# A causal attention stage with routing: from half items of eight heads to one whole item a step

## The reference

```
x = x + self_attention(norm(x))                     # stage 1, causal, 16 heads of 16
x = x + cross_attention(context, norm(x))           # stage 2
x = x + _L0_ffn_ref(norm(x), ...)                   # stage 3: the one that is changed
x = x + rotation_attention(norm(x)); x = x + wide_cross(norm(x)); x = x + moe(norm(x))   # stages 4 to 6

def _L0_ffn_ref(x, ...):
    q_in = k_in = rope(x)                           # r1 = x1*cos - x2*sin, r2 = x1*sin + x2*cos, on neighbours
    q, k, v = q_in @ Wq.T + bq, k_in @ Wk.T + bk, x @ Wv.T + bv
    attn = softmax(causal(q k^T / 4))               # 16 heads of 16, 100 x 100 for each of 32 items
    x1 = layer_norm(x + (attn v) @ out_proj.T + b, ln1_w, ln1_b)
    gates = softmax(x1 @ gate_w.T + gate_b); top_idx = top 2 of 8
    moe_out = sum over the two of gate * (x1 @ expert_w.T + expert_b)
    return layer_norm(x1 + moe_out, ln2_w, ln2_b)
```

## Time and profile before

| what | us |
|---|---|
| median of three runs | 3509.99 |
| lowest and highest | 3508.03, 3511.72 |
| profiled execution, own time | 3483.03 |
| profiled execution, span | 3481.2 |
| PE busy | 3282.1 (94%) |
| DVE busy | 1841.8 (53%) |
| ACT busy | 1636.2 (47%) |
| POOL busy | 1556.1 (45%) |

### The profile page before, as it was taken

One profiled execution on the slowest core, in us unless ns is written; L12 is line 12 of the kernel. 1 busy time (PEld: TensorE's weight loads), 2 busy tenths in 40 slices (PEclk: granted clock), 3 DMA queues, 4 the chain that ended last, 5 costly groups with the idle time before them and its releaser, 6 DMA issues. The chain is left out here.

```text
span 3481.2 us, 70336 instructions
## 1 busy us (share of the span) xinstructions
PE 3282.1 (94%) x26012; PEld 2362.2 (68%) x26013; DVE 1841.8 (53%) x5751; ACT 1636.2 (47%) x3411; POOL 1556.1 (45%) x2142
## 2 busy tenths in 40 slices
PE   7997999988999769998899999999999989999998
PEld 5774566656666644444577777777777678899997
DVE  5664777756888546665445454554554456111114
ACT  4663666656776036776354555555445421111111
POOL 1002444435776244552466666666566656000017
PEclk9998999999999789999999999999999989999999
DMA  8501111100000540000100000000000002999973
GB/s 269 218 2 42 42 42 42 42 27 1 22 23 21 155 134 15 20 20 6 44 8 8 14 8 8 8 14 8 8 8 8 1 25 60 323 325 326 326 250 103
DMA packets 111487, 263.28 MB, mean 76 GB/s; under 512 B 24003, under 2 KB 70240, under 8 KB 95840
## 3 DMA queue, kind: packets, MB, share of 16 engines
q1 hardware_dynamic: 90208, 224.70, 20.0%
q0 software_dynamic: 16384, 26.29, 2.7%
q10 hardware_dynamic: 4608, 8.39, 0.6%
HBM read 196.61 MB, written 62.65 MB: 74 GB/s over the span
## 5 line engine op out<-in xcount | busy, mean ns | idle before, releaser
L2728 POOL TENSOR_SCALAR wide_probs<-wide_probs,wide_inverse 100x361 f32<-100x361 f32 x512 | 603.9, 1192 | 0.1
L2995 ACT ACTIVATE wide_probs<-wide_probs,wide_least 100x361 f32<-100x361 f32 x512 | 301.0, 592 | 7.4 <-DVE wide_least L3092 7.4
L3092 DVE CUSTOM_DVE_ANT_0 wide_probs<-banks,wide_bias 100x361 f32<-100x361 f32 x512 | 251.7, 529 | 45.4 <-issue 40.3
L2780 PE MATMUL banks<-w_wide_v,wide_c 64*120 64x512 f32 (+1 forms) x1152 | 266.3, 591 | 0.9 <-DVE wide_v L3078 0.9
L2392 ACT ACTIVATE rot_h<-banks,w_rot_b 128x800 f32<-128x800 f32 x256 | 223.6, 924 | 86.4 <-PE banks L2266 83.3
L2774 PE MATMUL banks<-wide_c,w_wide_k 64*128 64x361 f32 x1536 | 256.7, 466 | 7.4 <-DMA wide_c<-in_ctxT 7.4
L2726 POOL TENSOR_TENSOR wide_hold_pool<-eps 100x1 f32<-100x1 f32 x256 | 49.4, 193 | 456.3 <-DVE wide_inverse L3098 456.3
L3536 ACT ACTIVATE tiles_hT<-banks 128x512 f32<-128x512 f32 x114 | 68.1, 597 | 346.4 <-PE banks L3452 346.4
L2807 PE MATMUL banks<-wide_kT,wide_qT 64*100 64x361 f32 x1024 | 208.7, 479 | 8.3 <-DVE wide_least L3092 6.6
L3452 PEld LDWEIGHTS banks<-tiles_xT,tiles_w 128*128 128x128 f32 x1824 | 212.5, 192 | 4.5 <-issue 1.6
L2774 PEld LDWEIGHTS banks<-wide_c,w_wide_k 64*128 64x128 f32 x1536 | 150.2, 188 | 96.2 <-issue 9.7
(11 more groups left out here) (469 smaller groups left out, 7490.5 us busy)
## 6 DMA issues: line engine op xcount, KB each, us to landing
tiles_w<-in_moe_w SPq DMA_DIRECT2D x114, 1024.0 KB, 5.1
slots<-zeros SPq DMA_DIRECT2D x58, 512.0 KB, 5.5
cross_c<-in_ctxT SPq DMA_DIRECT2D x32, 270.8 KB, 4.3
wide_c<-in_ctxT SPq DMA_DIRECT2D x32, 270.8 KB, 4.0
mix_kT<-slots SPq DMA_DIRECT2D x32, 256.0 KB, 4.2
slots<-mix_kT ACTq DMA_DIRECT2D x32, 256.0 KB, 4.0
tiles_rows<-slots SPq DMA_DIRECT2D x57, 128.0 KB, 4.7
slots<-tiles_out SPq DMA_DIRECT2D x57, 128.0 KB, 4.9
```

The source lines that it names most:

```text
L2728: last = nc.gpsimd.tensor_scalar(t.probs[:, i, j, :], t.probs[:, i, j, :], t.inverse[:, i, j:j + 1], None, ALU.mult)
L2780: last = nc.tensor.matmul(make_bank(unit, lane)[0:kw, :], t.c[rows_of(lane), of.buf, k, k0:k0 + kw], w.v[rows_of(lane), k, of.hf * BANK:(o ...
L2995: last = nc.scalar.activation(t.probs[:, i, j, :], t.probs[:, i, j, :], ACT.Exp, bias=t.least[:, i, j:j + 1], scale=-1.0, accum_out=t.rows ...
L3092: last = nc.vector.tensor_tensor_reduce(t.probs[:, i, j, :], scores(j), t.bias[:, :], -1.0, LARGEST, ALU.add, ALU.min, t.least[:, i, j:j + 1])
```

## The change

`causal_phase` goes. `self_phase` stands as it was, and its local names become the module's (ITEM_ROUNDS is now ROUNDS). A new `mix_phase` is built in the manner of `self_phase`: a step works on one item n, `even` and `odd` steps alternate, and the lists are these (PE's whole, the others' cut):

```diff
-            def score(of, i): ...      # 4 units a pair: 2 masks, 2 matmuls over 64 rows
-            def run_mix(oldest, older, before, here, after, third): ...
+            def mask(b):
+                if b > 0:
+                    pe.wait_ge(s.shifted, b)
+                for r in range(RG):    # 4 banks
+                    nc.tensor.matmul(g.psum[0:S, r, 0:HEADS_OF_BANK * S], g.ident_b[0:S, 0:S], g.causal[:, :], start=True, stop=False)
+            def scores(b): ...         # 8 matmuls over 32 rows, 200 columns
+            def project(b):
+                pe.wait_ge(s.headsT, b + 1)
+                if b + 1 < B:
+                    pe.wait_ge(s.heads, b + 2)
+                ...
+            def turn_x1(p):
+                pe.wait_ge(z.x1, (p + 1) * LANES)
+                pe.wait_ge(s.k, min(p + 4, PAIRS))
+                ...
+            def place(p, n):
+                pe.wait_ge(z.counted, p + 1)
+                pe.wait_ge(s.headsT, min(n - 2, B))
+                pe.wait_ge(s.heads, min(n - 1, B))
+                ...
+            # even: scores(n) turn_first(n-1) turn_parts(n-2) make_rows(k+1) turn_last(n-1) project(n-3) parts_by_v(n-1)
+            #       make_rope(k+1) mask(n+1) make_q(k+1) turn_heads(n-2)
+            # odd:  scores(n) turn_first(n-1) turn_parts(n-2) make_k(k+1) turn_last(n-1) place(k-3) project(n-3) parts_by_v(n-1)
+            #       turn_x1(k-2) mask(n+1) make_v(k+1) turn_heads(n-2) gate(k-2)
```

DVE and ACT:

```diff
+            def step(n):                              # DVE
+                peak(n)
+                second_norm(n - 4)
+                divide(n - 2)
+                shift(n)
+                add(n - 3)
+            def even(k, n):
+                step(n)
+                stats(k + MIX_AHEAD)                  # MIX_AHEAD = 3
+                add_bias(k + 1)
+                choose(k - 3)
+            def odd(k, n):
+                step(n)
+                count(k - 3)
+                place(k - 3)
+                peak_gates(k - 2)
-    for block_of in blocks:                           # ACT: k in 4 blocks, 8 instructions a pair; now 2, 4 instructions
-                nc.scalar.copy(x1_pairs[:, of.pair, :], u.x1[:, of.buf, :, :].rearrange("s l d -> s (l d)"))
+                nc.scalar.activation(t.y[:, p % TURNS, lane, :], g.x[:, p * LANES + lane, :], ACT.Identity, bias=u.offset[:, lane, :], scale=m1.rstd[:, lane, :]).then_inc(s.y, 1)
```

POOL:

```diff
-                nc.gpsimd.tensor_tensor(b2[:, :, 0], y2[:, :, 1], sin2[:, :, 0], ALU.mult)
-                nc.gpsimd.tensor_tensor(b2[:, :, 1], y2[:, :, 0], sin2[:, :, 1], ALU.mult).then_inc(z.rope_parts, 1)
+                nc.gpsimd.tensor_tensor(b2, y2[:, :, ::-1], sin2, ALU.mult).then_inc(z.rope_parts, 1)
-                if not (of.fixed and of.pair == 0):
-                    pool.wait_ge(g.scattered, of.pair * 64 if of.fixed else pool.snap(of.pair * 64))
+            # even: second_root(n-4) rope(k+1, 1) first_norm(n-4), wait for ropeT of k+2, scatter(k-4, 0)
+            # odd:  second_root(n-4) roots(k+3) first_norm(n-4) rope(k+2, 0), wait for x1T of k-1, scatter(k-4, 1)
```

More of the change, by code:

```diff
@@ L118 @@
 TURNS = 3
[L119 to L122, removed]
+HEADS_OF_CHUNK = NH // DC
+EDGES = 2
 HEAD_ROWS = 32
 HEADS_OF_ROUND = P // HEAD_ROWS
-ROUNDS = HEADS_OF_UNIT // HEADS_OF_ROUND
-PROBS_RING = 2
+ROUNDS = NH // HEADS_OF_ROUND
+HEADS_OF_BANK = DC * EDGES
+BANKS_OF_TURN = 2
+HEADS_OF_TURN = BANKS_OF_TURN * HEADS_OF_BANK
+KEEP = 4
+MIX_AHEAD = 3
 WARM = 4
@@ L1070 @@
-EDGES = 2
-HEADS_OF_BANK = DC * EDGES
-BANKS_OF_TURN = 2
-HEADS_OF_TURN = BANKS_OF_TURN * HEADS_OF_BANK
-HEADS_OF_CHUNK = NH // DC
-ITEM_ROUNDS = NH // HEADS_OF_ROUND
 def self_phase(nc, g, w):
@@ L1083, in self_phase @@
         t = buffers(nc, ctx, "self", y=[S, TURNS, LANES, D], yT=[P, DC, LANES, S], qT=[P, TURNS, DC, LANES, S], kT=[P, TURNS, DC, EDGES, LANES, S], v=[S, TURNS, LANES, NH, HD + 1],
-                    rowmax=[S, 2, NH], probs=[S, 2, NH, S], probsT=[S, NH, S], parts=[P, ITEM_ROUNDS, S], rowsum=[S, 2, NH], heads=[S, 2, D], headsT=[P, DC, S], own=[P, EDGES])
+                    rowmax=[S, 2, NH], probs=[S, 2, NH, S], probsT=[S, NH, S], parts=[P, ROUNDS, S], rowsum=[S, 2, NH], heads=[S, 2, D], headsT=[P, DC, S], own=[P, EDGES])
         m1 = norm_of(nc, ctx, "self_ln")
@@ L1090, in self_phase @@
         parts_bank, make_bank, out_bank = g.psum[:, 4, :], g.psum[:, 6, :], g.psum[:, 7, :]
-        parts_out = parts_bank[:, 0:ITEM_ROUNDS * S].rearrange("p (r s) -> p r s", r=ITEM_ROUNDS)
+        parts_out = parts_bank[:, 0:ROUNDS * S].rearrange("p (r s) -> p r s", r=ROUNDS)
         heads_out = out_bank[0:S, :].rearrange("s (h d) -> s h d", d=HEAD_ROWS)
@@ L1205, in parts_by_v @@
                 pe.wait_ge(s.v, p + 1)
-                for r in range(ITEM_ROUNDS):
+                for r in range(ROUNDS):
                     for j in range(HEADS_OF_ROUND):
@@ L3827, in decoder @@
             mix_w["expert_b"] = weight_as(mix_stack, "mix_b", "mix_expert_b", [P, NE * D], i["mix_expert_b"].rearrange("e d -> (e d)").unsqueeze(0).broadcast_to([P, NE * D]))
-            causal_phase(nc, g, mix_w, True)
+            mix_phase(nc, g, mix_w)
             mix_stack.close()
```

1446 lines of the change are left out of this document (618 added, 828 removed).

## The result

| what | us |
|---|---|
| median after (four runs, 3482.0 to 3493.4) | 3489.11 |
| median before beside it (four runs) | 3510.05 |
| ratio, 95% interval | 0.9939 (0.9924 to 0.9954) |
| profiled execution after, own time and span | 3493.37, 3491.2 |
| the same two kernels in a later batch, other chip | 3470.90 and 3483.48, ratio 0.9958 (0.9944 to 0.9973) |

The change is faster, by 0.4 to 0.6%: 12.6 to 20.9 us, where 13 were forecast. The 3489.11 us lie at the lower end of the forecast's span of 3489 to 3503.

The account below looks back on a forecast made before the run. PE bounds the mix stage (20.34 of 21.0 us busy), DVE 3 us behind. Loop -15.6, head +1.8, tail +1 and tile half 0 give -12.8 us: 3510 to 3497, span 3489 to 3503, range 3471 to 3518.

Parts of the forecast that it names:

- The loop through `divide`: Mix stage: PE's place and project wait for DVE's division, so DVE binds; 19.68 us a pair, 20.60 with blocking.
- two of its signs: Mix stage: a steady pair of 20.2 to 21.0 us; PE idle 1 to 3 us before `place` in odd steps.
- the even chain: DVE's even step in the mix stage: peak, second norm, shift, add, stats, add_bias and choose, 9.92 us in all.
- Blocking 0.92 us a pair: Mix stage's even chain: DVE held up by POOL through their shared port; 0.92 us, bounds 0 and 3.1.
- Rival 2: Even chain: second norm, add_bias and choose each blocked, 3.1 us; pair 22.8 us, whole 3526; chance 0.13.
- its point of decision, 1.9 us: Even chain: blocking a pair from which the slower rival decides, 12.8 / 13 more than 0.92.
- rival 1: Mix stage: DVE finishes its even chain in time and PE binds at 18.25 us a pair; -41, 3469; chance 0.14.
- Early pairs: Mix stage's pairs 0 to 2, without routing: about 15, 17 and 18 us, 50 together.
- Head +1.8: Stage's start to first scores: one bank, roots before rope, make_v first, fewer k copies; +1.8 us, between 0 and 4.
- Tail +1: Last subtraction to first tile load, routing the last pairs: 40 us against 39.1, +1, between -3 and +6.
- The reversed pair: POOL's exchanged rope product as one instruction of 256 columns: 0.74 us, up to 1.95 without effect.
- Own time: Whole kernel: profiled execution of 3483.03 us taken as 27 below the runs' median, becoming 3470.

Follow-up runs that it names:

- e3: Changed kernel with VectorE's division placed before the second norm in both steps, no work added or removed: 3464.07 us, ratio to before 0.9942.
- e2: Changed kernel with the first norm's statistics moved from VectorE's even step to the end of its odd step: 3458.95 us, ratio to before 0.9927.
- e9: Changed kernel with add_bias moved back from VectorE to GpSimd's even step, behind first_norm: 3462.52 us, ratio to before 0.9930.
- e7: Changed kernel with e2, e3 and e6 together, plus pair 0's rope items ahead of pair 1's roots on GpSimd: 3484.10 us, ratio to before 0.9930.
- e5: Changed kernel with GpSimd's first_norm products behind the wait for ropeT, so beside VectorE's add_bias and choose: 3501.00 us, ratio to before 0.9967.
- e11: e7 plus, on ScalarE in the head, pair 1's first norm behind the copy of pair 0's rope: 3449.73 us, ratio to before 0.9893.
- e6: Changed kernel with tail scatters not waiting for ropeT or x1T, two of them moved behind item 31's first norm: 3491.06 us, ratio to before 0.9944.
- e1: Changed kernel unchanged, run again as yardstick and for a second profile: 3470.90 us.
- e12: Changed kernel unchanged, run again on a later batch's chip as yardstick: 3469.73 us.
- e10: Changed kernel with rope's exchanged product split into two operations on strided halves instead of one with a reversed pair: 3468.45 us.
- e4: Changed kernel with GpSimd's even-step scatters ahead of rope and first_norm, no longer waiting for ropeT: 3471.25 us.

## Why the prediction came out as it did

- **The loop through `divide`: right,** though two of its signs were missed: the pair takes 19.49 us and not 20.2 to 21.0, and PE waits 0.55 us before `place` and not 1 to 3. Place and releaser are as laid out; e3 shows it without a change of work, e2 and e9 by taking work from the even chain, e7 by ending it. Without blocking the sum was 19.68 us, measured 19.49: the even chain 9.49 instead of 9.92 (add_bias 0.64 for 0.82, stats 0.93 for 1.02, shift 1.73 for 1.81) and the odd part 10.00 instead of 9.76.
- **Blocking 0.92 us a pair: mis-sized, it is 0.** This is the largest term that was off: 12 x 0.92 = 11.0 of the 12.4 us by which pairs 3 to 14 beat the forecast (232.8 us against 245.2). I took the amount from choose before and assumed choose beside POOL's roots, second_norm beside rope and add_bias beside scatters would suffer the same. They don't, as long as the products lie beside peak and shift. e5 puts first_norm's two back and gets 0.76. I also misread where the 0.92 came from: half of it is L920 beside a scatter's issue, against my sentence that issues don't stretch the rows of choose that they meet. Rival 2 (slower by blocking) names the right danger; its point of decision, 1.9 us, was not reached even in e5.
- **PE binds (rival 1): false here,** true once the even chain is relieved (its even step, which the prediction put at about 8.3 us, is 8.16 by its own terms, but no sum used it); it then gives 18.46, where 18.25 was worked out. That PE's own list got shorter is what the change gains from (20.34 us busy in 21 before); which of its parts shortened it, the 16-head steps, the score matmuls over 32 rows or the fewer hand-overs, no run separates.
- **Early pairs** took 17.9, 17.0 and 18.7 us by their even peaks, not 15, 17 and 18: 3.5 more, which makes the loop's -25.6 of what would have been -29.
- **Head +1.8: measured +4.6,** beyond my bound of 4. The roots of the second pair before rope were counted at 1.3 and cost 3 (first rope product 7.1 us after the stage's start instead of 4.1), as they themselves wait for statistics and for ScalarE. PE's turn of rope comes 2.6 us later for it. The other 2.0 lie between that turn and the first scores, where 0.9 was priced: the makes of q and k took 6.1 us of PE at a granted clock of 0.50 to 0.52 (790 to 800 us), against 4.5 in the kernel before at 0.73 and more, and the forecast had nothing for that. e11 gives 4.0 of the head back.
- **Tail +1: measured +6.6,** beyond the bound of 6. I used the steady steps' lengths, which are lengths at full clock. The growth lies ahead of the last first norm: from the last subtraction's start to that norm's end it takes 30.2 us instead of 23.0, and from there to the first tile load 17.3 instead of 17.1. e6 shows that scatters are only a small part. The granted clock from the last subtraction's end to that norm's end was 0.74 before and 0.64 after. In e1 it was 0.55 and the tail 2.8 us longer, but in e12 it was 0.58 and the tail that of the first profile, so how much of the growth is clock and how much order stays open; it wasn't tried.
- **The reversed pair: right,** 0.72 us; e10 shows it to be worth 2 us in the loop.
- **Own time.** The forecast took a profiled execution 27 us below the median as a constant offset. It is the standstill at the end, which an execution has or has not; the two runs' batches without it give -12.6 and -17.4, the one with it -20.9.

The errors, 10.0 us too little gain in the loop and 8.4 too little loss in head and tail, cancel: the forecast of -12.8 stands beside -14.4 in the two first profiles (-12.0 to -19.4 over all of them) and -12.6 to -20.9 in the runs. That the total came out so near is luck; the mechanism of the loop is not.

## What to carry to other kernels

When a pipeline is cut into steps, look for the step in which one engine's list is longer than the other engines', and move work out of it before shortening anything: 1 us moved between two steps (e2, 0.76 a pair) gave as much as 1.3 us moved to another engine (e9, 0.69). Set the two-operand work of GpSimd beside VectorE's passes over PSUM (e5 against the changed kernel). Beside VectorE's additions in SBUF DMA issues cost nothing here, but keep them away from its operations of a tensor with scalars (L101 in e4, L920 before). Price head and tail from the order in which their first and last results pass the engines, at the clock granted there, not from steady lengths.

## What was not expected of the hardware

- A VectorE norm of one tensor operand in SBUF (L101) waited for a GpSimd scatter issue beside it (0.79 us for 0.41, e4), and so did the small comparison with a scalar in the kernel before (L920, 0.65 us for 0.17), while add_bias (0.73 us for two) and the additions and comparisons of two tensors in choose kept their lengths (0.29 us) beside such issues.
- On some chips, executions of both kernels stand still for 24 to 26 us in the last 125 us, with ScalarE waiting up to 28.8 us at a time and matmuls coming one by one; on others none did. One profile was taken of each kernel in each batch, so this rests on five executions with the standstill and nine without.
